# A sixteen-head attention pipeline on one core: scores issued for two heads at a time, and two groups of turns moved ahead of a matmul group

## The reference

```
x  = layernorm0(x + up(expert(gelu(down(x)))))              # adapter with an expert chosen per sample
x1 = layernorm(x) * (1 + scale) + shift                     # scale, shift from the time step
q, k, v = x1 @ Wq + bq, x1 @ Wk + bk, x1 @ Wv + bv          # 16 heads of 16 channels
scores  = q k^T / 4 + attention_bias[b, h]                  # 256 x 256 for each head
probs   = softmax(where(mask, -inf, scores))
x2 = x1 + (probs @ v) @ Wo + bo
x3 = x2 + ffn(layernorm(x2) * g2 + beta2)                   # 256 -> 1024 -> 256, tanh form of x*sigmoid(1.702x)
x4 = layernorm(x3 + mlp chosen by the sample's kind)
out = max(x4 + dt * (finite differences of grids * x4), 0)  # first and second derivatives in both axes
```

## Time and profile before

| | us |
|---|---|
| runs, median of 3 (lowest to highest) | 876.44 (875.49 to 876.72) |
| the profiled execution | 875.6 |
| its span | 873.7 |
| PE busy | 810.6 (93% of the span) |
| VectorE busy | 738.0 (84%) |
| ScalarE busy | 621.9 (71%) |
| GpSimd busy | 164.5 (19%) |

### The profile page before, as it was taken

The page is one execution under the profiler, slowest core; times in us unless marked ns, Lnnn a source line. Parts: engine busy times, 40 slices in busy tenths (PEclk is TensorE's granted clock), DMA queues, the critical chain, the costliest instruction groups (busy, mean ns, idle before and its releaser), DMA issues.

```text
span 873.7 us, 18591 instructions
## 1 busy us (share of the span) xinstructions
PE 810.6 (93%) x5968; PEld 693.5 (79%) x5968; DVE 738.0 (84%) x2474; ACT 621.9 (71%) x1284; POOL 164.5 (19%) x160
## 2 busy tenths in 40 slices
PE   5593899999999999999999999999999999999992
PEld 2472578888888888888888898888888888887782
DVE  4744776898989989898989899898989899878787
ACT  2433767887978787887878787878879787677541
POOL 3210102212220303021122203021222212111020
PEclk9967999999999999999999999999999999999996
DMA  5467578577685867576577857576766757574100
GB/s 175 130 191 215 128 182 186 144 181 179 156 194 139 185 151 187 156 173 163 166 180 173 174 153 177 150 194 148 185 161 154 193 146 174 137 177 127 50 31 24
DMA packets 147593, 137.33 MB, mean 157 GB/s; under 512 B 19282, under 2 KB 144787, under 8 KB 147492
## 3 DMA queue, kind: packets, MB, share of 16 engines
q1 hardware_dynamic: 146532, 135.28, 62.2%
q10 hardware_dynamic: 960, 0.79, 0.5%
HBM read 98.23 MB, written 4.23 MB: 117 GB/s over the span
## 4 chain that ended last, share of the span: by engine, by line
PE 82%; DVE 9%; issue 4%; SPq 3%; ACT 1%; ACTq 1%; POOL 0%; DMA 0%; DVEq 0%; POOLq 0%
PE back_bank L1359 12%; PE turn_bank L1315 12%; PE context_bank L1369 7%; PE score_bank L1555 7%; PE score_bank L1556 6%; PE front_bank L1353 5%; PE attend_bank L1353 5%; PE back_bank L1353 5%; PE front_bank L1408 3%; PE back_bank L1339 3%; PE back_bank L1330 3%; PE attend_bank L1339 3%; PE front_bank L1661 2%; PE attend_bank L1300 2%; PE attend_bank L1377 2%
## 5 line engine op out<-in xcount | busy, mean ns | idle before, releaser
L560 ACT ACTIVATE sc<-sc,negmax 128x256 f32<-128x256 f32 x512 | 231.2, 504 | 26.2 <-DVE negmax L1191 25.4
L1191 DVE CUSTOM_DVE_ANT_0 sc<-score_bank,side 128x256 f32<-128x256 f32 x512 | 195.2, 418 | 50.5 <-PE score_bank L1556 34.4
L554 ACT ACTIVATE pt<-turn_bank 128x512 f32<-128x512 f32 x176 | 105.7, 601 | 136.2 <-PE turn_bank L1315 108.6
L1315 PE MATMUL turn_bank<-ident,sc 128*128 128x128 f32 x1024 | 156.4, 276 | 1.3 <-ACT sc L560 1.3
L1315 PEld LDWEIGHTS turn_bank<-ident,sc 128*128 128x128 f32 x1024 | 123.2, 141 | 31.8 <-issue 13.9
L1555 PE MATMUL score_bank<-ks,qs 128*128 128x256 f32 x512 | 123.4, 323 | 3.9 <-issue 3.8
L1359 PE MATMUL back_bank<-w,ffT 128*128 128x256 f32 x512 | 118.5, 379 | 0.4 <-DVE ffT L1100 0.4
L1359 PEld LDWEIGHTS back_bank<-w,ffT 128*128 128x128 f32 x512 | 96.8, 190 | 13.4 <-DVE ffT L1100 1.0
L480 POOL TENSOR_TENSOR rstd<-var,half_neg 128x2 f32<-128x2 f32 x64 | 50.8, 794 | 283.9 <-DVE var L953 282.4
L1556 PE MATMUL score_bank<-mask_neg,ident_r 128*128 128x512 f32 x256 | 102.6, 401 | 0.0
L1555 PEld LDWEIGHTS score_bank<-ks,qs 128*128 128x128 f32 x512 | 79.2, 194 | 12.0 <-issue 10.7
(11 more groups left out here) (246 smaller groups left out, 1956.3 us busy)
## 6 DMA issues: line engine op xcount, KB each, us to landing
side<-in_side SPq DMA_DIRECT2D x128, 512.0 KB, 5.2
qs<-qh SPq DMA_DIRECT2D x128, 64.0 KB, 4.1
qs<-ql SPq DMA_DIRECT2D x128, 64.0 KB, 4.2
ks<-kl SPq DMA_DIRECT2D x124, 64.0 KB, 4.1
ks<-kh SPq DMA_DIRECT2D x120, 64.0 KB, 3.9
wb<-in_wb SPq DMA_DIRECT2D x15, 512.0 KB, 6.5
xN<-in_x SPq DMA_DIRECT2D x16, 256.0 KB, 4.4
wc<-in_wc SPq DMA_DIRECT2D x16, 256.0 KB, 2.8
```

Source lines behind the costliest of these rows:

```text
L554: e.activation(pt[:, h % NP2, :, :], two(tbank[h % 2]), ACT.Copy).then_inc(copied[h % 4], 1)
L560: i = e.activation(sc[:, h % NS, q, :], sc[:, h % NS, q, :], ACT.Exp, bias=negmax[:, q, h:h + 1], scale=-1.0)
L1191: i = e.tensor_tensor_reduce(sc[:, s % NS, q, :], two(sbank[s % 2])[:, q, :], side[:, (H * X.i + s) % NSIDE, q, :], -1.0, 3.4e38, ALU.add, ...
L1315: i = e.transpose(tbank[h % 2][:, k * S + q * P:k * S + q * P + P], sc[:, h % NS, q, k * P:k * P + P], ident[:, :])
```

## The change

The first three instructions of a slot on PE (two score matmuls and the mask) become a function `score(x, h)`. It is called only in even slots, for heads s and s+1 in a row. Odd slots no longer begin with scores. The wait for `biased` of head h-2 is in the function, so that in slot s PE now waits for VectorE's work on head s-1 as well. In slot 3 the turns of head 1 stand ahead of `differ(U, 1)`, and in slot 11 those of head 9 ahead of the group on `w1`; both groups are in the short format and were ahead of the turns. No instruction is added or removed; VectorE, ScalarE, GpSimd and SyncE run the same instructions in the same order.

```diff
+            def score(x, h):
+
+                head(e, biased, x, h - 2)
+                for q in range(TT):
+                    e.matmul(two(sbank[h % 2])[:, q, :], qs[:, h // 2, q * P:q * P + P], ks[:, h, :], start=(q == 0), stop=False)
+                i = e.matmul(sbank[h % 2][:, :], ident_r[:, :], mask_neg[:, x.par, :, :], start=False, stop=True)
+                i.then_inc(scored[h % 4], 1)
+
...
-                    if X:
+                    if X and s % 2 == 0:
                         if s % HM == 0:
                             e.wait_ge(ld_stack[s // HM], times(X, STACKED))
-                        head(e, biased, X, s - 2)
                         if s == 0:
                             e.wait_ge(ev["mask_ready"], X.n)
-                        for q in range(TT):
-                            e.matmul(two(sbank[s % 2])[:, q, :], qs[:, s // 2, q * P:q * P + P], ks[:, s, :], start=(q == 0), stop=False)
-                        i = e.matmul(sbank[s % 2][:, :], ident_r[:, :], mask_neg[:, X.par, :, :], start=False, stop=True)
-                        i.then_inc(scored[s % 4], 1)
+                        score(X, s)
+                        score(X, s + 1)
...
                         if T:
                             e.wait_ge(ev["x3_ready"], T.n)
                             turn(bbank, x3, ev["x3_turned"])
+                        four(flip)
                         if U:
                             differ(U, 1)
-                            four(flip)
-                        else:
-                            for n in range(4):
-                                flip(n)
...
                     elif s == 11:
+                        for n in range(4):
+                            flip(n)
                         if B:
                             wait(e, ev["x4_ready"], B.p)
                             e.wait_ge(ev["n3l_ready"], B.n)
                             project_T_parts(bbank, w1, w1l, 0, n3h, n3l, 2, ev["w1_done"])
-                        for n in range(4):
-                            flip(n)
```

## The result

| | before | after |
|---|---|---|
| median of the runs (lowest to highest), us | 876.58 (875.49 to 877.38) | 903.88 (902.57 to 907.37) |
| span of the profiled execution, us | 873.7 | 900.8 |
| PE busy | 810.6 (93%) | 821.5 (91%) |
| VectorE busy | 738.0 (84%) | 737.5 (82%) |
| one period, samples 3 to 13 | 48.37 | 50.13 |

The ratio of after to before is 1.032 (95% interval 1.028 to 1.035): 27 us slower. The forecast was 900.0 with a range of 882 to 907. PE's busy time grows by 10.9 us although it runs the same matmuls. A mask counts as 0.40 us busy and the next matmul normally starts 0.24 us after it; ahead of a wait nothing runs beside its last 0.16 us, and the score pair behind a wait, whose weight load had waited too, takes 0.34 us up to its mask instead of 0.24. VectorE's busy time does not grow.

A forecast was written before the change was run, and what follows sets the result against it. PE was taken to bound the steady part, with VectorE only 4 us behind. Twelve periods at 1.7 us make 20.4, plus 1 and 3 for the ends 24.4, on 875.6 gives 900.0 us; range 882 to 907.

The forecast's parts named there:

- What bounds the kernel: Steady part: PE busy for all 48.40 us of a period; VectorE, busy 44.15, is full and late in the second half.
- Format: Scores on PE: grouping them to change formats less often saves 0, bounds 0 and 0.08 us per step.
- The rival that read 0.08 from one row: Scores behind transpositions: each step into the short format costs 0.08 us, so the kernel gets faster, 868 us; chance 0.05.
- Step 1: Slot 8 to 9, `v_ready`: values and copy come 0.48 us late, and PE waits 0.48 at the turn of `xN`.
- Step 2: Slot 10, `n3`: head 11's scores add 0.48 us ahead of its turn, so VectorE's `n3l` is 0.96 late.
- Step 3: Slots 11 to 15: full VectorE gives nothing back; PE waits some 0.5 us in slot 12, at no extra cost.
- Step 4: Slot 0: head 1's scores wait for VectorE's head 15, leaving PE 1.63 us late, earlier delays included.
- Step 5: Slots 3 to 5: `differ(U, 1)` ends 0.44 us later, making PE's gather loads 0.1 late.
- The period: Steady part of the changed kernel: periods of about 50.1 us, some 1.7 more per period.
- More harm: Rival: turns behind waiting scores become late too, VectorE loses another 0.5 us per period in slots 12 to 15, 907 us; chance 0.10.
- The ends: First and last samples: 1 us for samples 0 and 1, 3 us (bounds 1 and 5) for samples 14 and 15.

The follow-up runs named there:

- interleave: Kernel before, with the four transpositions of a turn in slots 11 to 14 run among the short-format matmuls on `w1`: 877.36 us, ratio 1.0009.
- pairs_only: Changed kernel without the moved turns, so the short-format groups in slots 3 and 11 stand ahead of the turns again: 902.46 us, ratio 1.0286.
- turns_only: Kernel before with only the turns moved ahead of the short-format groups in slots 3 and 11, one head scored per slot: 876.66 us, ratio 1.0003.
- no_pair_0_8_10: Changed kernel with two heads scored only in slots 2, 4, 6, 12 and 14, moved turns kept: 881.44 us, ratio 1.0058.
- pairs_2_4_6: Kernel before with two heads scored in slots 2, 4 and 6 only, turns where they were: 877.58 us, ratio 1.0012.

## Why the prediction was right, point by point

- **What bounds the kernel.** PE in the steady part, with VectorE full from slot 9 to slot 15: right. With the three pairs undone VectorE does the same work in a period of 48.47, so its rate is not the bound; with only slot 0's undone (49.45) the delays of slots 8 and 10 still count in full, so it gives nothing back.
- **Format.** Saving taken as 0 with a bound of 0.08 us per step: measured 0.002 by interleave. The rival that read 0.08 from one row had its answer in the row before.
- **Step 1.** 0.48 predicted; from the turn to `xN` 0.95 us instead of 0.47; undoing it gives 0.51 per period.
- **Step 2.** 0.96 predicted. From the first score of slot 8 to `n3l` are 9.31 us instead of 8.33, 0.98 more. VectorE idles 0.80 of it; 0.11 it was late by already, and 0.08 because `n3l` used to begin while the last read-out of head 10 still ran. Undoing the pair gives 0.50.
- **Step 3.** Some 0.5 of waiting in slot 12 predicted: measured 0.42 between the starts and 0.10 more in the scores behind the wait. That it costs nothing extra was shown from the other side: pairs_only fills 0.4 of it with another wait and is not slower.
- **Step 4.** 1.63 predicted as the sum of what PE loses up to the second score of slot 0. The starts give 0.47 (`xN`) + 0.52 (slot 12) + 0.67 (slot 0) = 1.66. Undoing slot 0 takes 0.68 from the period. One term is right by luck: the sum took 0.15 us for a waiting PE to start after VectorE, a figure read off a wait for ScalarE. Measured it is 0.06 (496.74 to 496.80), and the scores behind the wait take 0.10 longer, which the sum did not have.
- **Step 5.** 0.1 predicted for the gather; the periods of turns_only and no_pair_0_8_10 are 0.11 and 0.10 longer, and 0.08 of it stands right before the gather (0.52 for 0.44).
- **The period.** 50.1 predicted, 50.13 measured.
- **More harm.** This rival did not come true in the steady part: from `n3l` to the end of head 15 VectorE is without idle time (0.04 us at most before a row), and the period is 50.13, not 50.6.
- **The ends.** This term was too small. Spans compared: up to the start of sample 1 0.2 us, sample 1 1.05, sample 2 2.74, samples 3 to 13 19.2 (eleven times 1.75), sample 14 2.31, the rest 1.58; together 27.1, predicted 24.4. Samples 0 and 1 were put at 1 (measured 1.2), sample 2 at the steady 1.7 (2.74: the same collision stands in the changed kernel's trace at 156.05, where VectorE's instruction took 1.55 us), the eleven steady ones at 1.7 each (1.75, 0.5 more in all), samples 14 and after at 3 (3.9). The largest miss was to price sample 2 as a steady sample, although it is the first with T in work and still without U. GpSimd's addition for T meets VectorE's L974 there, which made VectorE 1.06 us later; how the rest of the 2.74 us comes about stays open.

## What to carry to other kernels

In a pipeline where each engine runs its queue in order, putting a block of 0.5 us one slot earlier makes everything that stands behind it in that slot 0.5 us later. What another engine makes from that, and hands back in the next slot, loses 0.5 us of cover. List those hand-overs and their cover before such a move. A hand-over with no cover delays the engine that waits, and every engine further on that has no idle time passes the delay on in full. The reuse of a buffer that was due one slot later can become a wait even when the buffer's reader is the faster engine on average, if the reader is late in that part of the period. Pairs were free in the steady part where the reader had caught up (slots 2, 4 and 6), but in samples 2 and 14, with other work in the slots, PE waited at pairs of slots 4, 12 and 14. So such a move is better made slot by slot than by a rule, and its ends are priced by themselves.

## What the runs showed of the hardware

- Alternating float32 transpositions and float32r matmuls costs 2 ns per step in and out (interleave). The record of a matmul that follows a transposition starts 0.08 us early (0.02 to 0.03 behind it instead of 0.11) and lasts 0.08 us longer (0.36 for 0.28); only the distance over both is time.
- The scores behind a wait for VectorE start 0.06 us after the read-out's end and take 0.34 us up to their mask, in a row of matmuls 0.24 (slots 12 and 0 of the changed kernel).
- A VectorE instruction on two SBUF operands (L974, 128 x 256, a product and a sum) and an addition on GpSimd (L500, 128 x 512) held each other up. Whichever began first went through in its usual time, and the other took longer: 1.54 for 0.48 us on VectorE where the records overlap for 1.26 us (pairs_2_4_6), or 1.59 for 1.28 on GpSimd where they overlap for 0.44 (kernel before). A change in the order of the two starts, from 37 ns behind to 17 ns ahead, thus made VectorE 1.06 us later in a start-up sample. The Trainium skill (SBUF — State Buffer, "SBUF: two separate sides") says that the two share a port pair, which is a lock that the one that starts first holds for its whole instruction. Both traces agree as to who is held up, though the growth is 0.13 to 0.20 us less than the recorded overlap.
